# Cross attention: the scores of four heads issued together, with one set of score banks instead of two halves

## The reference, cut to what matters

```python
q = x @ Wq.T + bq            # 100 x 256
k = ctx @ Wk.T + bk          # 361 x 256
v = ctx @ Wv.T + bv
s = q_h @ k_h.T / sqrt(16)   # each head: 100 x 361
p = softmax(s)               # over the 361 keys
x = layernorm(x + concat(p @ v_h) @ Wo.T + bo)
```

## Time and profile before

| | |
|---|---|
| median of 3 runs | 2338.49 us (2338.36 to 2340.51) |
| the profiled execution's own time | 2342.73 us |
| its span in the profile | 2341.1 us |
| TensorE busy, share of the span | 2062.2 us, 88% |
| VectorE busy | 1312.6 us, 56% |
| ScalarE busy | 1121.2 us, 48% |
| the cross attention's scores | first at 495.1 us, last at 878.9 us |

### The profile page before, as it was taken

One profiled execution on the slowest core, in us unless ns is written; L12 is line 12 of the kernel. 1 busy time (PEld: TensorE's weight loads), 2 busy tenths in 40 slices (PEclk: granted clock), 3 DMA queues, 4 the chain that ended last, 5 costly groups with the idle time before them and its releaser, 6 DMA issues. The chain is left out here.

```text
span 2341.1 us, 48582 instructions
## 1 busy us (share of the span) xinstructions
PE 2062.2 (88%) x17426; PEld 1283.4 (55%) x17427; DVE 1312.6 (56%) x3201; ACT 1121.2 (48%) x2443; POOL 516.1 (22%) x599
## 2 busy tenths in 40 slices
PE   4888888789999996799989999999999999964993
PEld 2555555546666664566545555555555555552762
DVE  4788888535555553477835555555555555541224
ACT  2777776525555551277724444544444444420110
POOL 5677677111010001266510000000000000003002
PEclk8999999769999996899989999999999999977996
DMA  5000000022110000000000000000000000044102
GB/s 167 2 2 0 0 0 2 2 70 73 68 45 24 13 7 1 1 1 0 1 13 7 7 7 6 6 6 6 6 6 12 7 6 1 1 165 169 33 29 66
DMA packets 50376, 60.85 MB, mean 26 GB/s; under 512 B 9761, under 2 KB 44886, under 8 KB 49830
## 3 DMA queue, kind: packets, MB, share of 16 engines
q1 hardware_dynamic: 47278, 53.74, 7.4%
q0 software_dynamic: 3008, 5.91, 0.8%
HBM read 51.11 MB, written 8.52 MB: 25 GB/s over the span
## 5 line engine op out<-in xcount | busy, mean ns | idle before, releaser
L2367 ACT COPY la_pT<-la_pPT 128x400 f32<-128x400 f32 x246 | 122.0, 496 | 258.0 <-PE la_pPT L2120 257.5
L2089 PE MATMUL la_side<-la_wkv,la_inT 128*128 128x512 f32 (+1 forms) x512 | 243.9, 599 | 0.0
L2077 PE MATMUL la_side<-la_inT,la_wkv 128*128 128x461 f32 x512 | 225.5, 564 | 0.9 <-ACT la_inT L2342 0.8
L2257 DVE CUSTOM_DVE_ANT_0 la_pr<-la_pS,la_mb 100x461 f32<-100x461 f32 x256 | 148.2, 636 | 130.0 <-PE la_pS L2107 130.0
L2431 POOL TENSOR_TENSOR la_xb<-io_X,la_bo 100x256 f32<-100x256 f32 x16 | 11.7, 730 | 784.2 <-DVE io_X L2246 784.2
L2358 ACT ACTIVATE la_pr<-la_pr,la_nm 100x461 f32<-100x461 f32 x256 | 172.5, 681 | 0.0
L2120 PEld LDWEIGHTS la_pPT<-io_ident,la_pr 100*128 100x128 f32 x984 | 110.5, 142 | 102.3 <-issue 97.4
L1081 DVE TENSOR_REDUCE ca_nm<-ca_pS 100x2 f32<-100x722 f32 x128 | 116.2, 908 | 90.0 <-PE ca_pS L968 88.2
L2219 DVE COPY la_v<-la_side 128x512 f32<-128x512 f32 (+1 forms) x128 | 88.3, 690 | 131.0 <-PE la_side L2089 129.6
L1153 ACT ACTIVATE ca_pr<-ca_pS,ca_nm 100x361 f32<-100x361 f32 x256 | 130.0, 561 | 64.7 <-DVE ca_nm L1081 62.8
L2120 PE MATMUL la_pPT<-io_ident,la_pr 100*128 100x100 f32 x984 | 125.9, 250 | 1.1 <-issue 1.1
(11 more groups left out here) (360 smaller groups left out, 4256.6 us busy)
## 6 DMA issues: line engine op xcount, KB each, us to landing
rf_w<-in_L_ffn_W SPq DMA_DIRECT2D x16, 1024.0 KB
ca_cn<-in_ctx SPq DMA_DIRECT2D x16, 256.0 KB
far_cn<-in_ctx SPq DMA_DIRECT2D x16, 256.0 KB
rows_in<-io_zero SPq DMA_DIRECT2D x20, 128.0 KB, 1.8
rb_xr<-rows_in POOLq DMA_DIRECT2D x20, 128.0 KB, 2.3
rows_out<-rb_yr SPq DMA_DIRECT2D x20, 128.0 KB, 1.7
ea_wcT<-in_t_L_ffn_conv_W SPq DMA_DIRECT2D x1, 2048.0 KB
la_wkv<-in_L_xattn_Wkv SPq DMA_DIRECT2D x1, 2048.0 KB
```

What stands on the lines that cost most here:

```text
L2077: last = nc.tensor.matmul(pf[:, 0:SK], wkv[:, k, e * P:(e + 1) * P], inT[:, k, :], start=k == 0, stop=k == KD - 1)
L2089: last = nc.tensor.matmul(pf[0:keys[c], :], inT[:, k, c * P:c * P + keys[c]], wkv[:, k, o:o + 512], start=k == 0, stop=k == KD - 1)
L2257: ins = nc.vector.tensor_tensor_reduce(out=pr[m % 4][:, e, 0:SK], in0=pS[0:T, 2 * (m % 2) + e, 0:SK], in1=mb[b][:, :], scale=-1.0, scalar= ...
L2367: nc.scalar.copy(pT[m % 2][:, e, :], src[:, 0:NC * T]).then_inc(s_PT, 1)
```

## The change

The loop over eight pairs becomes a loop over MQ = 4 slots, each with two pairs m = 2j and m + 1. TensorE issues the scores of both pairs one behind the other, four heads on all four row tiles, into all four banks. The wait of scores on s_P is made once per slot, for all exponentials issued so far: the four banks are one buffer. In the slot, TensorE then issues: side step, turn(n-2), side step, turn(n-1), side step, values (of pairs n-4 and n-3), side step, where n is the even pair of the slot. VectorE issues both maxima first, then the first side read, evac of n-2, the other side reads. ScalarE issues (sums in slot 2,) the first side read, exps(m), the second side read, exps(m+1), evac of n-1, rstd in slot 3, the other side reads. Side steps are those of both pairs, in the same order: slot 0 has fx, fc0, fc1, fq; slot 1 fk0, fk1; slot 2 fv1, bo, bp; slot 3 by, fv0. The instructions and their shapes are the same.

```diff
-                    above(pe, s_P, n - 1)
+                    if m % 2 == 0:
+                        above(pe, s_P, n)
...
-                    for m in range(MP):
-                        n, small = i * MP + m, side.steps(i, m)
+                    for j in range(MQ):
+                        m, n = 2 * j, i * MP + 2 * j
+                        small = side.steps(i, m) + side.steps(i, m + 1)
...
                         scores(i, b, m)
+                        scores(i, b, m + 1)
                         between()
-                        if m >= 2 or not first:
+                        if j or not first:
                             turn(n - 2, (m - 2) % MP)
                         between()
-                        if m >= 5 and m % 2:
-                            values(n - 4, i, b, m - 4)
-                        elif m % 2 and not first:
-                            values(n - 4, i - 1, 1 - b, MP - 4 + m)
+                        if j or not first:
+                            turn(n - 1, (m - 1) % MP)
+                        between()
+                        if j > 1:
+                            values(n - 3, i, b, m - 3)
+                        elif not first:
+                            values(n - 3, i - 1, 1 - b, MP - 3 + m)
+                        between()
...
                         maxima(i, m)
-                        small = side.steps(i, m)
+                        maxima(i, m + 1)
+                        small = side.steps(i, m) + side.steps(i, m + 1)
                         for name, k in small[:1]:
                             step(name, k, i + 1 if name[0] == "f" else i - 1, 1 - b)
-                        if m % 2 == 0 and (m or not first):
-                            evac(n - 2, i * MQ + m // 2 - 1, (m - 2) % MP)
+                        if j or not first:
+                            evac(n - 2, i * MQ + j - 1, (m - 2) % MP)
...
+                        if j == 2 and not first:
+                            sums(i - 1)
                         for name, k in small[:1]:
                             step(name, k, i + 1 if name[0] == "f" else i - 1, 1 - b)
-                        if m == 4 and not first:
-                            sums(i - 1)
                         exps(i, m)
-                        if m % 2 and (m >= 3 or not first):
-                            evac(n - 2, i * MQ + (m - 1) // 2 - 1, (m - 2) % MP)
-                        if m == MP - 1 and not first:
+                        for name, k in small[1:2]:
+                            step(name, k, i + 1 if name[0] == "f" else i - 1, 1 - b)
+                        exps(i, m + 1)
+                        if j or not first:
+                            evac(n - 1, i * MQ + j - 1, (m - 1) % MP)
+                        if j == MQ - 1 and not first:
                             rstd(i - 1)
-                        for name, k in small[1:]:
+                        for name, k in small[2:]:
                             step(name, k, i + 1 if name[0] == "f" else i - 1, 1 - b)
```

More of the change, by code:

```diff
@@ L1091, in body @@
                     first = isinstance(i, int) and i == 0
-                    for m in range(MP):
-                        n = i * MP + m
+                    for j in range(MQ):
+                        m, n = 2 * j, i * MP + 2 * j
                         maxima(i, m)
-                        small = side.steps(i, m)
+                        maxima(i, m + 1)
+                        small = side.steps(i, m) + side.steps(i, m + 1)
                         for name, k in small[:1]:
                             step(name, k, i + 1 if name[0] == "f" else i - 1, 1 - b)
-                        if m % 2 == 0 and (m or not first):
-                            evac(n - 2, i * MQ + m // 2 - 1, (m - 2) % MP)
+                        if j or not first:
+                            evac(n - 2, i * MQ + j - 1, (m - 2) % MP)
                         for name, k in small[1:]:
                             step(name, k, i + 1 if name[0] == "f" else i - 1, 1 - b)
-                        if m == MP - 1 and not first:
+                        if j == MQ - 1 and not first:
                             normed(i - 1)
```

## The result

The changed kernel takes 2366.77 us (median of 4 runs, 2364.82 to 2368.22) against 2339.5 us for the kernel before beside it (4 runs, 2338.36 to 2342.74): a ratio of 1.0118, 95% interval 1.0103 to 1.0133. It is 27 us slower. I had forecast 2342.5 us and a range up to 2353.

A forecast was written before the change was run, and what follows sets the result against it. TensorE's own instructions bound the kernel; its saving would become waits. +2.3 us over 15 batch boundaries, +1.6 last batch, 0 first: +3.9 on the profiled 2342.73, 2346.6, less 4.24 for the median: 2342.5 us, range 2332 to 2353.

The forecast's parts named there:

- what TensorE saves: Scores: four heads at once cost 0.83 us instead of 1.58 for two pairs, saving some 0.75 a slot, 3.0 a batch.
- the saving turns into waits: Whole batch: TensorE's 3 us saved become waits for the second turn, side reads and gate; net +0.15 us a batch.
- The second turn waits for VectorE: Slots 0 and 2: turn(n-1) waits until VectorE, after two maxima, evacuates the single pPT; about 1.3 us in slot 0.
- fq for ScalarE's read of fc1: Slot 0: fq needs fc1's bank, which ScalarE reads (0.46 us) only after its evacuation; slot 6.53 us.
- the gate binds in slot 1: Slot 1: the next scores wait for all exponentials of the slot, making the single set of banks bind; slot 6.09 us.
- the sum: Four slots' waits add to 24.23 us, plus 0.14 for the loop's end: 24.37 a batch against 24.22, clock 1.00.
- The clock: Rival: TensorE busy about 83% of the stage, clock 0.96, about +1 us a batch, 2355 to 2360; chance 0.09.
- self attention's window: Evidence on the clock: one window with 12.34 of 15 us busy has clock 1.00, the next with 12.48 has 0.96.
- The chain: Each slot's path of waits between engines, followed from its scores; slot 0 puts the second turn at 3.62 us.
- the ends: First batch taken as 0, between -2 and +3 us; last batch 21.1 us against 19.5, +1.6.

The follow-up runs named there:

- the filled gap: Changed kernel plus twelve unread transposes where TensorE idles in slot 0: 2339.31 us, ratio 1.0012 to the kernel before.
- the reads reordered: Changed kernel with TensorE's values moved into its waits and fc1, fk1 read by ScalarE in another order: 2324.12 us, ratio 0.9947.
- the transposes at the end of slot 3: Changed kernel plus twelve unread transposes behind the values and last side step of slot 3: 2359.51 us, ratio 1.0090.
- the maxima undone: Changed kernel with VectorE's evacuation of the first turn back between the two maxima, ahead of the side reads: 2389.3 us, ratio 1.023.
- the hold: Changed kernel plus two unread VectorE reductions (1.1 us) between the maxima of slot 3, no added TensorE work: 2382.12 us, ratio 1.0185.

## Why the prediction was wrong

**Right: what TensorE saves.** 0.83 us for four heads was taken; it is 0.79 to 0.80. Right: that the saving turns into waits. The slots at full clock are 6.6, 6.0, 5.5 and 6.1 to 6.2 us; the forecast said 6.53 (more at a loop's turn), 6.09, 5.47 and 6.14. The second turn waits for VectorE, fq for ScalarE's read of fc1, the gate binds in slot 1, as said. A batch of 24.1 to 24.3 against 24.37. With the clock held (the filled gap) the ratio to the kernel before is 1.0012, and the forecast was 1.0017.

**Wrong: the clock.** The step that failed is that the sum holds clock 1.00 through the stage and so puts the clock's cost at nothing; over the 14 batches the mean is 0.92. The rival *The clock*, which should have caught it, was wrong in both its terms. Its chance of 0.09 rested on "the idle stretches here are about 1.3 us each", on self attention's window at the same share and clock 1.00, and on what the Trainium skill (TensorE: Matmul & The Clock Gate, HAM oscillation) has of long gaps; the trace does not agree with the way I used it. The stretch is 1.43 to 1.70 us, TensorE is busy 0.30 us in 2 in the longer kind, and the clock falls in nine batches of fourteen. The chain itself could have given the length: it has the second turn at 3.62 (3.65 in the batch from 595.72), and the scores, fx, the first turn and fc0 in front of it end 2.14 us after the scores go out (620.02 to 621.63 + 0.53); that leaves 1.5, and 0.18 more at the loop's turn. Its price was about 1 us a batch and "2355 to 2360"; it is 2.95 us a fall, 1.9 us as a mean over fourteen batches, and 2366.8. I had spread 8% of half clock evenly over the batch. It isn't spread: in the changed kernel the fall follows the thin stretch of slot 0, and so it meets fq, the scores and fk0 and fk1, which are the longest links of TensorE on the path. The mean clock of 0.96 in the row that I leaned on was too mild; a batch that falls has 0.87. And the same had shown both 1.00 and 0.96 at one share of busy time, which was the sign that the share doesn't decide, and that 0.09 was too sure.

**Wrong by less: the ends.** I gave the first batch 0 and the last +1.6. The first is 25.97 us instead of 28.99, 3.0 less; full clock came earlier, not later (clock 1.00 in the window from 510 to 525 against 0.88). I had also misread that window: the first batch starts at 495.07, not at 510, and stands at half clock through its first two slots, for 18.6 us and not 3.6.

```profile
495.07:513.62 18.55, 17.41 (x53) 9.32 (x52) 5.55 (x8) 5.51 (x12) 2.02 (x4) 0.50 0.62 174
```

The last batch runs in part at half clock and takes 23.5 us to its last turn but one instead of 19.6 (22.4 in the kernel with the filled gap).

**What stays open.** Why the clock falls in one batch and not in the next with the same instructions. Not the length of the gap alone: in the changed kernel all six of the longer gaps fall and three of the eight shorter, but with the reads reordered every second batch falls at one length of 1.4 us, with the transposes at the end of slot 3 three in fourteen at nearly the same length, and two gaps over 2 us a batch pass unharmed in most batches of the kernel with the maxima undone. Not the share of busy time (75% keeps the clock there, 91% of a full-clock batch loses it every second time where ScalarE's reads are reordered). Not the batch's length (the hold and the transposes make nearly the same length and nine falls against three). The Trainium skill (TensorE: Matmul & The Clock Gate, What's actually happening) says that the activity is counted over stretches that run on their own, not in step with the kernel. By that rule the same gap can fall whole into one stretch or be cut by its border; the strict alternation of two kinds of batch would suit it. No run here moved the work against those stretches and nothing else, so this is an argument and not shown.

## What to carry to other kernels

When a change takes work off the bounding engine and leaves its instructions in a chain of waits, add up the chain at full clock, and then look where TensorE's thinnest stretch comes to lie and which of its instructions stand right behind it: here standing still for 1.5 to 1.7 us cost 3 us in nine batches of fourteen. If the chain gives back all that was saved, the saving isn't lost; the freed time can be refilled by moving work that has slack (values, a late norm) into the wait, and by letting the engine that frees a shared bank read it first. A filler that nobody reads is a quick way to tell a loss of clock from a loss by waiting.

## What the runs showed of the hardware that I had not expected

- Scores of four heads on four row tiles cost TensorE 0.79 to 0.80 us, the same as two heads on two (0.79), not a little more.
- Two maxima back to back take 1.73 us (0.91 each alone).
- Six transposes of 100 columns, 0.6 us in a gap of 1.5 to 1.7 us, were enough to end nine falls and win about 26 us, each kernel measured against the one before in its own series; on the other hand a kernel with two gaps over 2 us in each batch, TensorE busy 75%, kept clock 1.00 in 11 batches of 14.
- A fall costs 0.8 to 1.1 us in slot 0 and 2.0 to 2.1 in slot 1 of the changed kernel, where fq, fk0 and fk1 are serial. Where the clock came back before slot 1, in two batches with the transposes at the end of slot 3, it cost 1.25 in all.
- The 0.18 us that VectorE spends at the loop's turn made TensorE's wait 1.70 instead of 1.52 us in every second batch, and all six of these fell.
